# Two-layer transformer kernel, second attention: stacks built by SBUF-to-SBUF transfers from two queues, q and k turned in the projection stage, six sets

## The reference

```python
qkv = jnp.clip(jnp.einsum('bsd,ed->bse', hidden_states, w_qkv), -CLIP_QKV, CLIP_QKV)
q, k, v = jnp.split(qkv, 3, axis=-1)
q = _layer_norm(q, q_ln_w, q_ln_b)          # over all 512 features, then scaled and shifted by feature
k = _layer_norm(k, k_ln_w, k_ln_b)
scores = jnp.einsum('bqhd,bkhd->bhqk', q, k) * scale + slopes[:, None, None] * rel
probs = jax.nn.softmax(jnp.where(causal, scores, -jnp.inf), axis=-1)
attn = jnp.einsum('bhqk,bkhd->bqhd', probs, v).reshape(B, S, D) @ w_out.T
```

## Time and profile before

| what | value |
|---|---|
| median of 3 runs | 2104.43 us (2103.82 to 2115.77) |
| profiled execution | 2108.64 us, span 2106.9 us |
| PE, DVE, POOL, ACT busy, of the span | 94%, 40%, 35%, 21% |
| projection stage, PE at work | 1396 to 1480.6 us |
| handover to the heads' stage | 1480.6 to 1489.7 us |
| warm-up, to the first score | 1489.7 to 1532.0 us |
| groups 0 to 7 | 1532.0 to 1863.5 us |

### The profile page before, as it was taken

One profiled execution on the slowest core, in us unless ns is written; L12 is line 12 of the kernel. 1 busy time (PEld: TensorE's weight loads), 2 busy tenths in 40 slices (PEclk: granted clock), 3 DMA queues, 4 the chain that ended last, 5 costly groups with the idle time before them and its releaser, 6 DMA issues. The chain is left out here.

```text
span 2106.9 us, 26188 instructions
## 1 busy us (share of the span) xinstructions
PE 1972.3 (94%) x10119; PEld 1537.1 (73%) x10119; DVE 849.1 (40%) x1580; ACT 451.9 (21%) x550; POOL 732.5 (35%) x974
## 2 busy tenths in 40 slices
PE   6999999999999999999998699989698899887998
PEld 5888888888888888888887588867444344356877
DVE  4242442423424424234244433136566566523332
ACT  3111111111111111111110201012145555532111
POOL 4332321313223213132000464348422332128775
PEclk9999999999999999999999799999679878897999
DMA  4010110010101100101001122010100000002333
GB/s 151 30 55 28 55 55 27 27 55 27 55 27 55 55 27 27 55 27 55 7 15 45 51 76 82 7 60 21 18 1 1 1 2 1 1 21 80 90 96 98
DMA packets 42817, 87.96 MB, mean 42 GB/s; under 512 B 12449, under 2 KB 17313, under 8 KB 38273
## 3 DMA queue, kind: packets, MB, share of 16 engines
q1 hardware_dynamic: 42752, 87.11, 12.9%
HBM read 84.86 MB, written 2.10 MB: 41 GB/s over the span
## 5 line engine op out<-in xcount | busy, mean ns | idle before, releaser
L146 PE MATMUL a_ps<-a_xh_h,a_w_h 128*128 128x512 f32 x768 | 307.3, 400 | 3.4 <-POOL a_w_l L270 2.0
L148 PE MATMUL a_ps<-a_xh_h,a_w_l 128*128 128x512 f32 x768 | 301.3, 392 | 0.0
L147 PE MATMUL a_ps<-a_xh_l,a_w_h 128*128 128x512 f32 x768 | 300.5, 391 | 0.0
L60 POOL TENSOR_TENSOR tick<-neg_half 128x1 f32<-128x1 f32 x108 | 36.2, 335 | 657.9 <-PE a_ps L148 615.7
L390 DVE TENSOR_TENSOR x<-x,a_ps 128x1024 f32<-128x1024 f32 x64 | 78.2, 1221 | 261.3 <-PE a_ps L148 261.3
L1195 ACT ACTIVATE a1h_pr<-a1h_ps 128x1024 f32<-128x1024 f32 (+1 forms) x192 | 150.0, 811 | 154.3 <-PE a1h_ps L1336 128.8
L146 PEld LDWEIGHTS a_ps<-a_xh_h,a_w_h 128*128 128x128 f32 x768 | 145.0, 189 | 31.6 <-DVE a_xh_l L101 4.0
L148 PEld LDWEIGHTS a_ps<-a_xh_h,a_w_l 128*128 128x128 f32 x768 | 144.4, 188 | 30.3
L147 PEld LDWEIGHTS a_ps<-a_xh_l,a_w_h 128*128 128x128 f32 x768 | 144.9, 189 | 28.0
L1356 PE MATMUL a1h_ps<-a1h_KT,a1h_QT 64*128 64x512 f32 (+2 forms) x384 | 128.0, 472 | 17.5 <-DVE a1h_mx L1245 6.2
L1160 POOL TENSOR_SCALAR_AFFINE_SELECT a1h_pr<-a1h_pr 128x256 f32<-128x256 f32 x128 | 51.6, 406 | 261.0 <-ACT a1h_pr L1195 260.2
(11 more groups left out here) (194 smaller groups left out, 3996.5 us busy)
## 6 DMA issues: line engine op xcount, KB each, us to landing
a_raw<-in_a_wqkgv SPq DMA_DIRECT2D x30, 1024.0 KB, 5.0
f_raw<-in_f_w SPq DMA_DIRECT2D x64, 256.0 KB, 2.6
f_raw<-in_f_w SPq DMA_DIRECT2D x33, 320.0 KB, 2.9
a_raw<-in_a_wout SPq DMA_DIRECT2D x32, 256.0 KB, 5.0
a_cst<-in_a_cst SPq DMA_DIRECT2D x32, 129.0 KB, 2.1
a1q_raw<-in_a_wqkv SPq DMA_DIRECT2D x3, 1024.0 KB, 4.8
x<-in_x_in SPq DMA_DIRECT2D x8, 256.0 KB, 4.2
a_v_nat<-in_a_wqkgv SPq DMA_DIRECT2D x2, 1024.0 KB, 9.7
```

The source lines that it names most:

```text
L60: nc.gpsimd.tensor_tensor(top["tick"][:, :], top["neg_half"][:, 0:1], top["neg_half"][:, 1:2], ALU.mult)
L146: nc.tensor.matmul(out, w_hi, x_hi, start=start, stop=False)
L147: nc.tensor.matmul(out, w_hi, x_lo, start=False, stop=False)
L148: return nc.tensor.matmul(out, w_lo, x_hi, start=False, stop=stop)
```

## The change

In the projection stage q and k are turned while they are still whole: the feature weight and bias are now per partition. `TURNS` lists 16 units of four transposes (four token tiles, one block of 128 features) that PE makes behind projections 7 to 19 in the last two banks; ACT takes the high part, DVE the whole, POOL the difference. The projections have 6 banks instead of 8, the ring `cl` has 8 tiles instead of 4, and the weights of v are split one quarter at a time. The result is four tiles `turned` with features on partitions, and two tiles of slope rows.

In the heads' stage a stack is now filled by transfers of 16 rows of 4 KB from `turned`, and of slope rows: 20 for each of the first six pairs, on SP for `KTs` and on ACT for `QT`, and 16 for each of the other ten, all on SP. `gather`, `turn` and the copies on ACT are gone. SETS is 6, SLOTS is 3. The order of the pieces alternates wide and narrow ones. The warm-up takes in 8 pieces of pair 2 (AHEAD), and a maximum row now follows two pieces into the next pair. Values come in halves, one behind each score.

```diff
+TURNS = [(m, 8 * c + 4 * half, b) for c, half, m in ((0, 0, 7), (0, 1, 10), (1, 0, 14), (1, 1, 18)) for b in range(KT)]
+TURNS = [(m + b // 2, first, b) for m, first, b in TURNS]
...
-        R = 4
+        R = 8
+        PROJ = 6
...
+            def low(u):
+                pool.wait_ge(s("full"), u + 1)
+                nc.gpsimd.tensor_tensor(target(u, "_l"), full[:, u % 2, :], target(u, "_h"), ALU.subtract
+                                        ).then_inc(s("turned_lo"), 1)
...
+            for i in range(2):
+                split_hi(nc.gpsimd, slopes[i][:, :], raw_slopes[i]).then_inc(s("slopes_round"), 1)
+            for m in range(QK):
+                moments(m)
+                for u in units(m):
+                    low(u)
+                if m in (9, 11, 12, 13):
+                    if m == 9:
+                        pool.wait_ge(s("proj_done"), NT)
+                    split(2, ((9, 11, 12, 13).index(m),))
...
+            def turn(u):
+                _, first, feature = TURNS[u]
+                pe.wait_ge(s("normed"), first + 4)
+                if u >= 2:
+                    pe.wait_ge(s("full"), u - 1)
+                for i in range(4):
+                    last = nc.tensor.transpose(ps[:, PROJ + u % 2, i * P:(i + 1) * P],
+                                               cl[:, (first + i) % R, feature * P:(feature + 1) * P],
+                                               top["ident"][:, :])
+                last.then_inc(s("turned"), 1)
...
-                else:
+                if m >= NT:
                     pe.wait_ge(s("w_split"), KT * (m // NT + 1))
-                    pe.wait_ge(s("clipped"), m - 7)
+                if m >= PROJ:
+                    pe.wait_ge(s("clipped"), m - PROJ + 1)
                 for k in range(KT):
                     part(m, k)
+                for u in units(m):
+                    turn(u)
...
+PIECES = [(4, 0, BANK, False), (0, 0, P, True), (5, 0, BANK, False), (4, 1, P, True),
+          (6, 0, BANK, False), (1, 0, 2 * P, True), (7, 0, BANK, False), (5, 1, 2 * P, True),
+          (3, 0, BANK, True), (2, 0, 3 * P, True), (7, 1, BANK, True), (6, 1, 3 * P, True)]
...
-        SETS, SLOTS = 5, 4
+        SETS, SLOTS = 6, 3
...
+        def stack(queue, p, kind):
+            tiles, parts = ((KTs, ("k_h", "k_l", "k_h")), (QT, ("q_h", "q_h", "q_l")))[kind]
+            to, landed = tiles[p % SETS].bitcast(F32), s(f"stack_in{p % SETS}")
+            if kind and p < SETS:
+                queue.wait_ge(s("set_clear"), p + 1)
+            for h in range(2):
+                e, r = 2 * p + h, ROWS * h
+                block, first = divmod(e * DH1, P)
+                for n, part in enumerate(parts):
+                    at = r + AUG + n * DH1
+                    queue.dma_start(to[at:at + DH1, :], turned[part].bitcast(F32)[first:first + DH1, block, :]
+                                    ).then_inc(landed, 16)
+                if kind == 0:
+                    queue.dma_start(to[r:r + 2, :], slopes[0].bitcast(F32)[2 * e:2 * e + 2, :]).then_inc(landed, 16)
...
+            def stack_both(p):
+                if p < PAIRS:
+                    g, i = divmod(p - SETS, 2)
+                    sp.wait_ge(s("score_made"), score_at(g, NS - 1, i) + 1)
+                    for kind in range(2):
+                        stack(sp, p, kind)
...
+            stack(sp, 0, 0)
+            sp.dma_start(mask[:, :], a["a1_mask"]).then_inc(s("mask_in"), 16)
+            sp.dma_start(later[:, :], a["a1_later"]).then_inc(s("later_in"), 16)
+            for p in range(1, SETS):
+                stack(sp, p, 0)
+            max_row(0)
+            max_row(1)
+            for g in range(QUADS - 1):
+                if g:
+                    stack_both(2 * g + 4)
+                max_row(2 * g + 2)
+                if g:
+                    stack_both(2 * g + 5)
+                max_row(2 * g + 3)
...
+            for p in range(SETS):
+                stack(act, p, 1)
             nc.scalar.copy(identb[:, :], ident[:, :]).then_inc(s("later_ready"), 1)
...
-                    if n == 1 and g:
+                    if n == 0 and g:
                         take_output(g - 1, 1)
-                    if n == 5:
+                    if n == 4:
                         take_output(g, 0)
...
                     score(g, n, i)
-                    if u == 0:
-                        turn(2 * g + 3)
-                    for _ in range(upto - made):
+                    for _ in range((upto - made + 1) // 2):
+                        next(strand)
+                    before = (u - 3) // 2
+                    if before >= 0:
+                        values(g, before, (u - 3) % 2)
+                    elif g:
+                        values(g - 1, NS + before, (u - 3) % 2)
+                    for _ in range((upto - made) // 2):
                         next(strand)
```

More of the change, by code:

```diff
@@ L1029, in counted @@
     pieces(0, 0, NP)
     pieces(1, 0, 2)
-    other("row", 0)
+    count("row", 0)
     pieces(1, 2, NP)
+    pieces(2, 0, 2)
+    count("row", 1)
+    pieces(2, 2, AHEAD)
     for g in range(QUADS):
-        for n in range(NS):
-            score(g, n, 0)
-            if n == 0:
-                turned(2 * g + 3)
-            score(g, n, 1)
-            if n == 7:
-                turned(2 * g + 4)
         p, q = 2 * g + 2, 2 * g + 3
-        pieces(p, 0, 2)
-        other("row", 2 * g + 1)
-        pieces(p, 2, 18)
+        pieces(p, AHEAD, 16)
@@ L1045, in counted @@
         if g:
-            other("out", g - 1, 1)
-        pieces(p, 18, NP)
+            count("out", g - 1, 1)
+        pieces(p, 16, NP)
         pieces(q, 0, 2)
         if p < PAIRS:
-            other("row", p)
-        pieces(q, 2, 10)
-        other("out", g, 0)
-        pieces(q, 10, NP)
-    other("out", QUADS - 1, 1)
-    return score_at, max_at
-SCORE_AT, MAX_AT = counted()
-def paced(g):
-    first = MAX_AT[("row", 2 * g + 1)] - (2 if g < QUADS - 1 else 0)
-    last = MAX_AT[("row", 2 * g + 3)] - 2 if g < QUADS - 2 else MAX_AT[("row", 2 * g + 3)] if g < QUADS - 1 else len(MAX_AT) - 1
-    worth = [PIECES[i[1]][3] + 80 if isinstance(i[0], int) else 300 for i in list(MAX_AT)[first:last]]
-    marks = [sum(worth[:i]) / sum(worth) for i in range(len(worth))]
-    length = 2 * sum(2 * n + 100 for _, _, n in STEPS)
-    upto, now = [], 1500
+            count("row", p)
@@ new lines, in counted @@
+        pieces(q, 2, 8)
+        count("out", g, 0)
+        pieces(q, 8, NP)
+        pieces(q + 1, 0, 2)
+        if q < PAIRS:
+            count("row", q)
+        pieces(q + 1, 2, AHEAD)
+    count("out", QUADS - 1, 1)
+    return at
+MAX_AT = counted()
+def paced(g):
+    if g == QUADS - 1:
+        return [0] * 3 + [1] * 9 + [2] * 12
+    items = list(MAX_AT)
+    first = MAX_AT[(2 * g + 2, AHEAD)]
+    last = MAX_AT[(2 * g + 4, AHEAD)] if g < QUADS - 2 else MAX_AT[("row", 2 * g + 3)] + 1
+    worth = [PIECES[i[1]][3] + 70 if isinstance(i[0], int) else 350 for i in items[first:last]]
+    length = sum(2 * n + 100 for _, _, n in STEPS) * 2
+    upto, now = [], 0
@@ L1071, in paced, with attention1_heads @@
             now += 2 * n + 100
[L1072 to L1076 removed]
+            upto.append(sum(sum(worth[:i]) * length < now * sum(worth) for i in range(len(worth))))
+    return upto
+def attention1_heads(nc, top, turned, slopes, v1, attn, a):
     ctx = ExitStack()
```

329 lines of the change are left out of this document (144 added, 185 removed).

## The result

The changed kernel takes 2047.99 us, the median of 4 runs (2045.52 to 2049.19), against 2110.1 us for the kernel before on the same chip, whose four executions lie between 2103.82 and 2130.37. The ratio is 0.968, 95% interval 0.964 to 0.972. The forecast was 2050 us. The profiled execution took 2049.02 us (span 2047.1).

What follows compares the result with a forecast made beforehand. PE was taken to bound the kernel, busy for 94% of the span, with DVE next in the groups. Eight terms summed to -54.5 us, from a profiled 2108.64 to 2054, median 2050 us; 8-in-10 range 2015 to 2085 us.

Steps and rivals of the forecast that it cites:

- Projection stage: Term 1: 7.0 us for transposes on PE, 2.3 for a new clip wait, 3.3 saved from an old one: +6.0 us.
- The other added work has cover: Projection stage: work added on POOL, DVE and ACT costs nothing in the sum; 2 us allowed in the range for POOL.
- Handover: Term 2, between projections and heads: 2.0 us left behind PE's last projection instead of 9.1, so -7.1 us.
- Warm-up: Term 3, heads' stage up to the first score: 36.4 us against 42.2 at 0.49 us an issue, so -5.8 us.
- My own upper bound of 0.64: Warm-up: dearer price of an issue, in us; the last issues end at 40 us and the term becomes nothing.
- rival D: Warm-up: slow transfers, at 95 GB/s, put the first score at 62.5 instead of 36.4 us; 2076 us; chance 0.08.
- Transposes, -26.9: Term 4, groups 0 to 6: the 208 transposes' 26.9 us of PE busy time all counts as time saved.
- Waits, -18.7: Term 5, groups: PE's waits go for the output copy (7.5 us), maximum row (3.6) and half of DVE's (7.6).
- Halved values, +10: Term 6, groups: values in halves cost 0.14 us more in each of 64 steps, 10 us at the stage's clock.
- Clock, -10: Term 8, groups: mean clock rises from 0.84 to 0.87 with the output copy's wait gone, 10 us less.
- rival B: Groups: the clock stays up as most falls come from vanishing gaps; 247 us instead of 284, 2013 in all; chance 0.12.
- terms 4 to 8: Groups: transposes -26.9, waits -18.7, halved values +10, eight pieces out of group 6 -2, clock -10 us.

Runs made afterwards that it cites:

- rows_first: Changed kernel with the maximum rows of pairs 0 and 1 issued on SP's queue ahead of K and Q stacks of pairs 4 and 5: median 2035.6 us.
- copy_late: Changed kernel with ACT's copy of the output bank one score later, as in the kernel before: groups 306.3 us, in all 2103.83 us.
- two_back: Changed kernel with the 13 blocks of 16 transposes put back and the output bank copied one score later: groups 306.4 us, in all 2100.37 us.
- whole_values: Changed kernel with each step's values in one piece, at the place of the first half: groups 259.7 us, in all 2054.65 us.
- old_pieces: Changed kernel with a pair's pieces in the order of the kernel before, DVE's wide ones together: groups 259.6 us, in all 2057.60 us.
- turns_back: Changed kernel with the 13 blocks of 16 transposes put back into groups 0 to 6: groups 267.1 us, in all 2064.28 us.
- one_block: rows_first with one block of 16 transposes ahead of the second score of group 0: groups 248.2 us, median 2033.79 us.
- warm_filler: rows_first with 36 transposes, one or two between PE's pieces in the warm-up: warm-up 59.0 us, groups 254.4 us, in all 2055.86 us.

## Why the prediction came out right, and where it was wrong

*Projection stage, +14.2 in place of +6.0: wrong.* The step that failed is "The other added work has cover". The wait of 2.3 us for the first clip came (2.1), and the old one of 3.3 went. What the step left out: the turn of a third unit waits for `full` of the first, 4.8 us in two places. For what brings such waits the runs point at POOL, which is late with the moments, but one wait for `full` stayed when POOL was relieved; I had looked at POOL for v's weights only. And each of the three gaps has 4 to 6 us at a clock of 0.59 to 0.72 behind it, 1.7 us each, which I had not counted; before, the one gap had cost 3.3 us in the same way. This makes 6.4 of the 8.2 us; another 1.2 is that the stage began with 8.0 us at half clock in place of 5.5, and rows_first, with 5.5 again, shows that to be chance.

*Handover, -7.4 in place of -7.1: right.*

*Warm-up, +12.2 in place of -5.8: wrong, and the largest single miss of a step.* The term that failed is the price of an issue, taken at 0.49 us and measured at 0.84 from one to the next. My own upper bound of 0.64 was about the undisturbed price (0.67); the rest is the contention that rival D spoke of, at 105 GB/s in place of its 95. I had seen that pair 0's row stands behind the stacks in SP's queue, and took it for harmless at 0.49. Rival D gave 62.5 us for the first score, measured 54.5. Pair 0's own stack was late as well: the first piece came 12.1 us after the first transfer (1504.4), where I had DVE start at 8.4.

*Transposes, -26.9.* As work it was exact (27 us). As time it was worth 14.2 in the changed kernel, and nothing in the one with the late copy.

*Waits, -18.7.* They went nearly as said: no copy, 0.9 us for a later row's transfer in place of 3.6, 8.0 us for DVE where 7.7 was left. POOL's triangle, for which up to 19 us were allowed, cost one wait of 0.5. *Halved values, +10* was the right price for PE's work and the wrong sign for the time: undone, the groups get 6.8 us longer.

*Clock, -10: wrong in size.* The mean rose to 0.94, out of the 0.82 to 0.92 that I had named, and is 1.00 from the second group to the seventh. The groups took 252.9 us, near rival B's 247, and B's mechanism is the one the runs bear out in the main: waits of about 1 us were put back in copy_late and the falls came back with them. Together terms 4 to 8 were 30.0 us short. That step rested on the mean clock of one group before, when the short stretches of the earlier trace rows already had the pattern: a level of 0.68 right behind a gap.

+8.2 and +18.0 against -30.0, and -0.3 in the handover: the sum missed by 4.1 us, and -1.2 us lie ahead of and behind the stages. The prediction was right as a number by luck, since its errors cancel; one of the signs by which I had said it would be wrong, the clock, did occur.

What stays open: undoing single parts gives 53.4 + 14.2 + 6.7 + 6.8 = 81.1 us, about the 77.6 won, but two_back shows that they do not add, so this is no account. Nor is it shown what separates a stretch at 0.50 in which PE is busy all the time from one in which it rises, nor why the clock fell in whole_values and old_pieces behind waits no longer than ones that left it at 1.00 elsewhere.

## What to carry to other kernels

Price a wait of the bounding engine with what follows it: in copy_late, in one execution, 22 us of waits cost another 31 us by low clock. In a queue, put what somebody waits for ahead of what merely must be done at some time; 62 issues of 0.84 us held a 4 KB row for 24 us. And when work is moved, list for each engine what it does in that stretch: the late one found in the projection stage was POOL, which the sum had looked at for v's weights only.

## What the runs showed of the hardware

On SP's queue a stack's transfers (copies of 16 rows of 4 KB within SBUF, and slope rows) followed each other every 0.67 us while ACT issued nothing, and every 0.84 or 0.85 while it did. In the first case a copy of 16 rows took 0.54 to 0.59 us to issue and one of 14 slope rows 0.83 or 0.84 (rows_first, 1537 to 1549 us).

The 208 transposes did not hold TensorE's clock down (0.99). With 16 in a row it rose 1.5 and 3.3 us after the first of them (turns_back, one_block), with 36 scattered ones not in 28 us (warm_filler).

Falls began behind single waits of 0.6 to 1.9 us in the kernel before and in copy_late. No length of a wait follows from that: a wait of 1.44 us left the clock at 1.00 once in copy_late, five falls in whole_values had no wait over 0.48 us ahead of them, and 28 waits of up to 0.4 us between 1580 and 1770 us left the changed kernel's clock at 1.00.
